# Third layer of a four-layer graph network: row factors spread by DMA instead of by TensorE transposes

## The chip, the cores and the metric

The kernel runs on 1 core of one Trainium2 chip. The metric is the device time in microseconds (us). Five engines work side by side, each with its own instruction stream: TensorE (PE in the profile, with PEld for its weight loads), VectorE (DVE), ScalarE (ACT), GpSimd (POOL) and SyncE (SP), which here only starts DMAs.

## The reference, cut to what matters

Sixteen graphs of 512 nodes with 128 features go through four attention layers, each followed by a residual sum and a layer norm. The third layer ("layer 2" in the names, L2 in the reference) has 8 heads of width 16:

```
e = leaky_relu(e_src[..., :, None] + e_dst[..., None, :], 0.2)
e = e + (beta * jnp.log(prior + EPS))[:, None, :, :]      # prior is the adjacency
e = jnp.where(adj > 0, e, neg_inf)
attn = softmax(e, axis=-1)
h = einsum('bhij,bhjf->bhif', attn, x_proj)               # 8 heads
return h.transpose(0, 2, 1, 3).reshape(B, N, D) @ W_out.T
```

The kernel never forms e. exp(leaky_relu(s_i + d_j)) is the larger of exp(s_i + d_j) and exp(0.2 (s_i + d_j)). After division by a factor that belongs to row i (it cancels in the softmax), a weight is max(R_i, T_j) times the mask, with R_i = exp(-0.8 (s_i + m)) and T_j = exp(0.8 (d_j - m)). A remaining factor of j is multiplied into the values. For each head one needs R as a row of 512 numbers that stands in all 128 partitions, since the nodes j lie along the partitions and the nodes i along the free dimension.

## The kernel before

Nodes lie as node = 4 p + c: 128 partitions, C = 4 columns of blocks. Everything is float32, but for the masks (bf16). Each stage is a small function of a graph `g` and a part; for each engine the string `ORDER[engine]` lists the stages as pairs of a letter and a graph number, and `turns` walks through it. So the order of work on every engine is written out as data, and an engine waits for its next stage even if a later one is ready. Four or five graphs are under way at once: while layer 0 of graph 9 runs, the same engines work on layer 1 of graph 8, layer 2 of graphs 7 and 6, and layer 3 of graphs 5 and 4. PSUM has 8 banks of 128 x 512; `BANK_OF_USE` gives the bank for each use, `wrote` and `took` are the waits for its being filled and emptied.

Layer 2 of one graph goes as follows:

- `l2_h` (TensorE, ScalarE) projects to 128 values and two scores for each of 8 heads. `l2_c4`, `l2_dm`, `l2_diag`, `l2_db` find the largest score m of each head, `l2_small` and `l2_cap` (VectorE) make the sums.
- `l2_e` (ScalarE, L758 to L760) makes R2 (the row factors, 128 x 32), t2e (the column factors T) and a factor for the values; `l2_scale` (GpSimd, L1292) multiplies the values by the latter.
- `l2_s` (TensorE, L561), once for each of 8 heads: four 128 x 128 transposes of a broadcast column of R2 spread the row factors of the head over all partitions of one PSUM bank.
- `l2_p` (VectorE, L1119), once for each head: four SCALAR_TENSOR_TENSOR of 128 x 512 make the weights P2 = max(row, T) x mask. P2 holds four heads, so head 4 waits for the product of the first four.
- `l2_v` (TensorE, L571), once for four heads: 16 matmuls of 128 x 512 with P2 as the moving operand. Then `l2_n`, `l2_rcp`, `l2_o`, `l2_oT`, `l2_y` normalise, project, and add the residual.

GpSimd does the elementwise work that needs no PSUM: `l0_bias` (L1229), `l1_y` (L1261), `scale` of the layers 1 and 3b (L1267), `l2_scale` (L1292), `below_zero` (L1274, `l3_min` on 128 x 1024 and `l3b_min` on 128 x 512), and after each layer norm's statistics four small instructions (`variance` L1237 and L1238, `power` L1245, `shifts` L1252) before ScalarE can normalise (L748). SyncE's queue starts one load of x (L398) and one store (L402) for each graph, in order, each after its wait.

## Time and profile before

| | |
|---|---|
| Device time, median of 3 runs | 1141.66 us (1140.52 to 1142.09) |
| The profiled execution: its own time, its span | 1140.98 us, 1139.2 us |
| Busy: PE, PEld, DVE, ACT, POOL | 1045.3, 782.5, 917.0, 736.3, 271.4 us |
| Mean TensorE clock granted | 0.977 of full |

The span runs from the first to the last instruction. Busy times are the union of an engine's instructions. A weight load overlaps the matmuls before it, so PE's busy time is what counts for the engine, with the idle time ahead of a group telling what it lacked. The profile names buffers without their numbers: `l_P` can be the weight matrix of layer 1 or of layer 3, and `bank` any PSUM bank.

### The profile page before, as it was taken

The numbers are of one execution on the slowest core, as the hardware profiler recorded it, in microseconds if no ns is written. First come the engines' busy times: TensorE is split into PE (matmuls) and PEld (weight loads), VectorE is DVE, ScalarE is ACT, GpSimd is POOL, SyncE is SP. The second block draws the span as 40 slices with busy tenths as digits, with TensorE's granted clock in tenths as the row PEclk, the third lists the DMA queues.
The fourth block names the chain that finished last, engine by engine and source line by source line (L and its number), as shares of the span: only waits on it lengthen the run. The fifth ranks groups of instructions, "written<-read, shape, count | busy, mean of one in ns | idle before, by whom it ended". The sixth has DMA issues, their size and how long they took to land. (4 is left out here: it accounts for less than half of the span.)

```text
span 1139.2 us, 26405 instructions
## 1 busy us (share of the span) xinstructions
PE 1045.3 (92%) x9333; PEld 782.5 (69%) x9333; DVE 917.0 (80%) x2514; ACT 736.3 (65%) x1901; POOL 271.4 (24%) x381
## 2 busy tenths in 40 slices
PE   2899999999999999999999999999999999879763
PEld 1567676877677767777787867777787768555552
DVE  4467999989897988979797997989797997977342
ACT  1699577757677684867678584867678584533522
POOL 0012212213131231413132141313132131421212
PEclk9999999999999999999999999999999999999877
DMA  4000000000000000000000000000000000000000
GB/s 120 1 11 12 11 2 11 1 11 11 10 2 12 10 11 11 11 11 11 11 2 11 10 11 11 11 11 11 11 1 11 2 11 2 10 1 10 10 0 19
DMA packets 9489, 12.97 MB, mean 11 GB/s; under 512 B 2704, under 2 KB 5008, under 8 KB 9232
## 3 DMA queue, kind: packets, MB, share of 16 engines
q1 hardware_dynamic: 9360, 11.28, 3.3%
q8 instruction: 77, 1.26, 0.5%
q14 instruction: 52, 0.43, 0.1%
HBM read 7.08 MB, written 4.19 MB: 10 GB/s over the span
## 5 line engine op out<-in xcount | busy, mean ns | idle before, releaser
L1119 DVE SCALAR_TENSOR_TENSOR P<-bank,t2e,mask_t 128x512 f32<-128x512 f32 x512 | 344.8, 739 | 19.1 <-PE bank L561 19.0
L703 ACT ACTIVATE probs<-probs,neg_max 128x512 f32<-128x512 f32 x256 | 184.8, 724 | 9.5 <-DVE neg_max L949 8.0
L748 ACT ACTIVATE x<-x,shift_l,rstd_l 128x128 f32<-128x128 f32 x256 | 105.6, 490 | 116.6 <-POOL shift_l L1252 116.4
L941 DVE CUSTOM_DVE_ANT_0 probs<-bank,mask_add 128x512 f32<-128x512 f32 x256 | 168.6, 677 | 15.3 <-PE bank L462 14.9
L713 ACT ACTIVATE probs_t<-bank 128x512 f32<-128x512 f32 x256 | 145.6, 614 | 10.4 <-PE bank L470 9.8
L470 PE MATMUL bank<-ident,probs 128*128 128x128 f32 x1024 | 139.6, 276 | 8.3 <-ACT probs_t L713 3.8
L470 PEld LDWEIGHTS bank<-ident,probs 128*128 128x128 f32 x1024 | 115.0, 141 | 28.9 <-ACT probs L703 15.2
L571 PE MATMUL bank<-P,GH 128*32 128x512 f32 x1024 | 119.7, 609 | 9.1 <-issue 8.2
L612 PE MATMUL bank<-t,l_P 128*128 128x257 f32 x512 | 121.2, 386 | 1.7 <-DVE l_P L1051 1.7
L612 PEld LDWEIGHTS bank<-t,l_P 128*128 128x128 f32 x512 | 94.6, 192 | 14.2 <-DVE l_P L1051 2.2
L571 PEld LDWEIGHTS bank<-P,GH 128*32 128x32 f32 x1024 | 32.2, 112 | 80.3 <-issue 78.9
L1274 POOL TENSOR_SCALAR e<-v 128x1024 f32<-128x1024 f32 x16 | 44.6, 2790 | 167.1 <-ACT v L795 155.7
L1237 POOL TENSOR_TENSOR rstd_l<-mv_l,ln_eps 128x4 f32<-128x4 f32 x64 | 12.8, 200 | 274.3 <-DVE mv_l L995 274.3
L539 PEld LDWEIGHTS bank<-t,l3b_P 128*128 128x128 f32 x512 | 63.5, 202 | 16.6 <-issue 10.1
L462 PE MATMUL bank<-head_k,head_q 32*128 32x512 f32 x512 | 73.7, 646 | 1.0 <-DVE row_max L941 0.5
L539 PE MATMUL bank<-t,l3b_P 128*128 128x129 f32 x512 | 67.6, 288 | 5.9 <-DVE l3b_P L1037 5.9
L1267 POOL TENSOR_TENSOR t<-t 128x512 f32<-128x512 f32 x32 | 33.4, 1045 | 150.0 <-ACT t L740 150.0
L539 PEld LDWEIGHTS bank<-t,l_P 128*128 128x128 f32 x512 | 59.6, 192 | 12.5 <-issue 10.9
L481 PEld LDWEIGHTS bank<-probs_t,v 128*32 128x32 f32 x2048 | 52.8, 110 | 21.9 <-issue 15.7
L1245 POOL TENSOR_TENSOR rstd_l<-rstd_l,neg_half 128x4 f32<-128x4 f32 x64 | 66.5, 1039 | 4.1
L481 PE MATMUL bank<-probs_t,v 128*32 128x128 f32 x2048 | 67.0, 275 | 0.5 <-issue 0.4
L561 PE MATMUL bank<-ident,R 128*128 128x128 f32 x512 | 66.0, 273 | 0.2
(161 smaller groups left out, 1944.2 us busy)
## 6 DMA issues: line engine op xcount, KB each, us to landing
x_in<-in_x SPq DMA_DIRECT2D x16, 256.0 KB, 3.0
out<-x SPq DMA_DIRECT2D x16, 256.0 KB, 2.0
l_P<-in_adj SPq DMA_DIRECT2D x1, 1024.0 KB, 5.1
w_fc<-in_L_gnn_W_fc SPq DMA_DIRECT2D x1, 256.0 KB, 3.5
probs_t<-in_L_gnn_a_fc SPq DMA_DIRECT2D x1, 256.0 KB, 5.6
w_cat<-in_L_gnn_W SPq DMA_DIRECT2D x2, 64.0 KB, 3.6
w3a<-in_L_gnn_mlp_w SPq DMA_DIRECT2D x1, 128.0 KB, 3.8
w3b<-in_L_gnn_mlp_w SPq DMA_DIRECT2D x1, 128.0 KB, 3.3
```

What stands on the lines that cost most here:

```text
L462: pe.matmul(ps("l0_s", g, HEADS0 * c + h)[:, :], g.of(head_q)[rows, c * P:(c + 1) * P], g.of(head_k)[rows, :], start=True, stop=True)\
L470: last = pe.transpose(ps[:, j * P:(j + 1) * P], probs[m // HEADS0 % 2][:, m % HEADS0, j * P:(j + 1) * P], ident[:, :])
L481: last = pe.matmul(ps[DH0 * h:DH0 * (h + 1), 0:P], g.of(v0)[:, j, DH0 * h:DH0 * (h + 1)], probs_t[c % 2][:, h, j, :], start=(j == 0), stop ...
L539: last = pe.matmul(ps[:, c * (D + 1):(c + 1) * (D + 1)], gat[n]["P"][:, j, (2 * k + c) * P:(2 * k + c + 1) * P], g.of(t)[:, j, 2:3 + D], s ...
L571: last = pe.matmul(ps[DH0 * h:DH0 * (h + 1), :], g.of(GH)[:, j, (GROUP2 * q + h) * W2:(GROUP2 * q + h) * W2 + DH0], P2[:, h, j, :], start= ...
L612: last = pe.matmul(ps[:, 0:HID + 1], gat["l3"]["P"][:, j, c * P:(c + 1) * P], g.of(t3)[:, j, 2:3 + HID], start=(j == 0), stop=(j == C - 1))
L703: act.activation(e, e, ACT.Exp, bias=neg_max[:, m:m + 1], scale=SCALE0, accum_out=g.of(den0)[:, m:m + 1])\
L713: act.activation(probs_t[c % 2][:, h, :, :].rearrange("p j n -> p (j n)"), ps("l0_t", g, m)[:, :], ACT.Copy)\
L748: last = act.activation(y[:, c, :], y[:, c, :], ACT.Identity, bias=shift[n][:, c:c + 1], scale=rstd[n][:, c:c + 1])
L941: dve.tensor_tensor_reduce(probs[c % 2][:, h, :], ps("l0_s", g, m)[:, :], mask_add[:, c, :], 1.0, -3.0e38, ALU.add, ALU.max, row_max[:, m: ...
L1119: last = dve.scalar_tensor_tensor(P2[:, h % GROUP2, j, :], ps("l2_s", g, h)[:, :], g.of(t2e)[:, j, h:h + 1], mask_t[:, j, :], ALU.max, ALU ...
L1245: pool.tensor_tensor(rstd[n][:, :], rstd[n][:, :], neg_half[:, :], ALU.pow)\
```

## The change

1. The stage `l2_s` is gone, with its 512 transposes and its 128 uses of a PSUM bank. In its place VectorE turns R2 in blocks of 32 x 32 (`l2_turn`, one instruction for each graph). SyncE's queue then writes the four blocks as 32 lines of 128 numbers to DRAM (`l2_rows`, four DMAs of 16 KB) and reads for each head 512 numbers back, once for every partition (`l2_spread`, eight DMAs of 256 KB into one of five buffers in SBUF, `row0` to `row4`). A head's spread waits for `l2_p` of five heads earlier.
2. `l2_p` reads the row factors from such a buffer in SBUF instead of from PSUM.
3. x3 has three buffers instead of two.
4. GpSimd's elementwise stages go in pieces of 128 columns: one instruction becomes four (eight for `l3_min`). The four small instructions of a layer norm stay as they are.
5. The order is new on all engines, and so are the banks.

```diff
+ROWS = 5
+BLOCK = 32
...
-        x1, x2, x3 = (pair(n, [P, C, D]) for n in ("x1", "x2", "x3"))
+        x1, x2, x3 = (pair(n, [P, C, D], n=k) for n, k in (("x1", 2), ("x2", 2), ("x3", 3)))
...
-        R2 = pair("R2", [P, HEADS2, C])
+        R2 = pair("R2", [P, HEADS2 * C])
+        turned2 = sb("turned2", [P, BLOCK])
...
+        rows = [sb(f"row{r}", [P, N_NODES]) for r in range(ROWS)]
...
+        line2 = [nc.dram_tensor(f"line2_{q}", [HEADS2 * C, P], F32, kind="Internal").ap() for q in range(2)]
...
+            def l2_rows(g, k):
+                sp.wait_ge(*sig("l2_turned", g, 1))
+                for q in range(0, P, BLOCK):
+                    sp.dma_start(g.of(line2)[:, q:q + BLOCK], turned2[q:q + BLOCK, :]).then_inc(signal["l2_rows"], 16)
+
+            def l2_spread(g, h):
+                if h == 0:
+                    sp.wait_ge(*sig("l2_rows", g, 64))
+                if HEADS2 * g.i + h >= ROWS:
+                    sp.wait_ge(signal["p2_made"], HEADS2 * g.i + h - ROWS + 1)
+                sp.dma_start(row(g, h)[:, :], g.of(line2)[h * C:(h + 1) * C, :].rearrange("c p -> (c p)")
+                             .rearrange("(o n) -> o n", o=1).broadcast_to([P, N_NODES])).then_inc(row_done(g, h)[0], 16)
...
-            def l2_s(g, h):
-                if h == 0:
-                    pe.wait_ge(*sig("exp2", g, 3))
-                ps = empty("l2_s", g, h)
-                for c in range(C):
-                    last = pe.transpose(ps[:, c * P:(c + 1) * P], g.of(R2)[:, h, c:c + 1].broadcast_to([P, P]), ident[:, :])
-                last.then_inc(filled("l2_s", g, h), 1)
...
-                pe.wait_ge(*took("l2_s", g, GROUP2 * q + GROUP2 - 1))
+                pe.wait_ge(*sig("p2_made", g, GROUP2 * (q + 1)))
...
+            def l2_turn(g, k):
+
+                dve.wait_ge(*sig("exp2", g, 1))
+                if g.has(1):
+                    dve.wait_ge(*sig("l2_rows", g, 64, back=1))
+                dve.transpose(turned2[:, :], g.of(R2)[:, :]).then_inc(signal["l2_turned"], 1)
+
             def l2_p(g, h):
-                dve.wait_ge(*wrote("l2_s", g, h))
+                dve.wait_ge(*row_done(g, h))
...
-                    last = dve.scalar_tensor_tensor(P2[:, h % GROUP2, j, :], ps("l2_s", g, h)[:, :], g.of(t2e)[:, j, h:h + 1],
+                    last = dve.scalar_tensor_tensor(P2[:, h % GROUP2, j, :], row(g, h)[:, :], g.of(t2e)[:, j, h:h + 1],
                                                     mask_t[:, j, :], ALU.max, ALU.mult)
-                last.then_inc(emptied("l2_s", g, h), 1)
+                last.then_inc(signal["p2_made"], 1)
...
-                    pool.tensor_scalar(e[:, :, :], v(g)[:, :, :], 0.0, None, ALU.min).then_inc(signal[n + "_min"], 1)
+                    for c in range(C):
+                        for q in range(0, e.shape[2], P):
+                            last = pool.tensor_scalar(e[:, c, q:q + P], v(g)[:, c, q:q + P], 0.0, None, ALU.min)
+                    last.then_inc(signal[n + "_min"], 1)
```

In the steady part of the program TensorE's rows change as follows. Before, the spreads of the row factors (L561, here of graph 7) stand between attention products of layer 3 (L612), of layer 3b (`l3b_P`) and the products of layer 2 (L571).

```order
495 L571 MATMUL bank<-P,GH 32x512 x16
496 L539 MATMUL bank<-t_0,l3b_P 128x129 x8
497 L553 MATMUL bank<-dmax_diag,ones 128x8
498 L612 MATMUL bank<-t_0,l_P 128x257 x4
499 L433 MATMUL bank<-ident,x_1 128x128 x4
500 L561 MATMUL bank<-ident,R_0 128x128 x4
501 L539 MATMUL bank<-t_0,l3b_P 128x129 x8
502 L462 MATMUL bank<-head_k,head_q 128x512 x4
503 L579 MATMUL bank<-ident,o_raw 128x128 x4
504 L561 MATMUL bank<-ident,R_0 128x128 x4
505 L612 MATMUL bank<-t_0,l_P 128x257 x8
506 L561 MATMUL bank<-ident,R_0 128x128 x8
```

Now, in the period of the same graphs (L592 is the product of layer 2, L633 the attention product of layer 3, L491 the scores of layer 0):

```order
450 L582 MATMUL bank<-dmax_diag,ones 128x8
451 L491 MATMUL bank<-head_k,head_q 128x512 x4
452 L556 MATMUL bank<-ident,l3b_R 128x128 x4
453 L592 MATMUL bank<-P,GH 32x512 x16
454 L462 MATMUL bank<-ident,x_1 128x128 x4
455 L633 MATMUL bank<-t_0,l_P 128x257 x4
456 L538 MATMUL bank<-w_cat,xTl 128x130 x2
457 L633 MATMUL bank<-t_0,l_P 128x257 x8
458 L491 MATMUL bank<-head_k,head_q 128x512 x4
```

The rows of L561 have no successor; the other stages are the same ones in another order.

On VectorE, before, the small sums of graph 7 (L1102 to L1107) are followed almost at once by the first weights P:

```order
805 L1102 TENSOR_TENSOR small<-t_0,dmax_all 128x32
806 L1103 TENSOR_TENSOR small<-t_0,dmax_all 128x32
807 L1107 TENSOR_SCALAR small<-small 128x32
808 L1145 RECIPROCAL l_rden<-bank 128x1
809 L1119 SCALAR_TENSOR_TENSOR P<-bank,t2e,mask_t 128x512 x4
```

Now the turn of the row factors (STREAM_TRANSPOSE) and other work stand between them:

```order
823 L1128 TENSOR_SCALAR small<-small 128x32
824 L1072 TENSOR_SCALAR l_P<-bank,l_g,l_b 128x512
825 L1136 STREAM_TRANSPOSE turned<-R_1 128x32
826 L1072 TENSOR_SCALAR l_P<-bank,l_g,l_b 128x512
827 L962 ISA probs,row_max<-bank,mask_add 128x512
828 L962 ISA row_max 128x1
829 L1058 SCALAR_TENSOR_TENSOR l3b_P<-bank,l3b_b,mask_t 128x512
830 L970 TENSOR_SCALAR neg_max<-row_max 128x4
831 L1058 SCALAR_TENSOR_TENSOR l3b_P<-bank,l3b_b,mask_t 128x512 x2
832 L1173 RECIPROCAL l_rden<-bank 128x1
833 L1058 SCALAR_TENSOR_TENSOR l3b_P<-bank,l3b_b,mask_t 128x512
834 L1173 RECIPROCAL l_rden<-bank 128x1
```

The next row is the first P of graph 7, from `row`. The last four heads of the graph stand later in the period, close together, with a layer norm of layer 1 started just ahead of them (BN_AGGR):

```order
888 L1016 BN_AGGR mv_l<-stats_l 128x2 x4
889 L962 ISA probs,row_max<-bank,mask_add 128x512
890 L962 ISA row_max 128x1
891 L1147 SCALAR_TENSOR_TENSOR P<-row,t2e,mask_t 128x512 x4
892 L1196 TENSOR_TENSOR x_0<-x_0,bank 128x512
893 L970 TENSOR_SCALAR neg_max<-row_max 128x4
894 L1147 SCALAR_TENSOR_TENSOR P<-row,t2e,mask_t 128x512 x4
895 L1202 SCALAR_TENSOR_TENSOR x_0<-x_0,x_1 128x512
896 L1147 SCALAR_TENSOR_TENSOR P<-row,t2e,mask_t 128x512 x4
```

SyncE's queue, which held one load and one store for each graph, now holds twelve DMAs more for each, in one line with them:

```order
66 L423 DMA line_0<-turned 32x32 x4
67 L430 DMA row<-line_0 128x512 x8
68 L418 DMA out<-x_1 128x512
69 L414 DMA x_in<-in_x 128x512
70 L423 DMA line_1<-turned 32x32 x4
71 L430 DMA row<-line_1 128x512 x8
```

## Rows read from the trace of the kernel before

**Rows 1.** Windows: each engine's busy time (its instructions), PEclk, DMA share, GB/s

```profile
0.00:200.00 200.00, 167.82 (x1708) 117.38 (x1709) 144.63 (x427) 136.64 (x363) 31.74 (x61) 0.99 0.09 24
200.00:960.00 760.00, 747.07 (x6875) 568.84 (x6874) 664.13 (x1819) 531.25 (x1376) 197.59 (x269) 1.00 0.03 9
960.00:1139.20 179.20, 130.37 (x755) 96.33 (x753) 108.23 (x270) 68.40 (x163) 42.03 (x52) 0.86 0.02 8
```

**Rows 2.** Windows: one period of the steady part, and another, later

```profile
398.00:462.70 64.70, 63.42 (x584) 48.29 (x583) 56.47 (x156) 45.69 (x119) 17.10 (x24) 1.00 0.03 10
...
656.80:721.50 64.70, 63.42 (x585) 48.25 (x583) 56.46 (x158) 45.69 (x120) 17.09 (x24) 1.00 0.03 10
```

**Rows 3.** Groups by line and form: busy us, mean ns | idle before, releaser

```profile
L1119 DVE SCALAR_TENSOR_TENSOR P<-bank,t2e,mask_t 128x512 f32<-128x512 f32 x512 | 344.8, 739 | 19.1 <-PE bank L561 19.0
...
L941 DVE CUSTOM_DVE_ANT_0 probs<-bank,mask_add 128x512 f32<-128x512 f32 x256 | 168.6, 677 | 15.3 <-PE bank L462 14.9
...
L561 PE MATMUL bank<-ident,R 128*128 128x128 f32 x512 | 66.0, 273 | 0.2
...
L1051 DVE TENSOR_SCALAR l_P<-bank,l_g,l_b 128x512 f32<-128x512 f32 x64 | 50.5, 795 | 1.5 <-PE bank L527 1.1 <-issue 0.4
L1037 DVE SCALAR_TENSOR_TENSOR l3b_P<-bank,l3b_b,mask_t 128x512 f32<-128x512 f32 x64 | 46.7, 743 | 2.8 <-ACT t L740 1.5 <-PE bank L527 1.3
...
L1145 DVE RECIPROCAL l_rden<-bank 128x1 f32<-128x1 f32 x64 | 10.4, 162 | 26.8 <-PE bank L612 26.7
```

**Rows 4.** Timeline (start us, us), VectorE and TensorE, two stretches

```profile
642.18 1.47 PE L561 MATMUL bank<-ident,R 128*128 128x128 f32 x12
...
647.30 2.72 DVE L1119 SCALAR_TENSOR_TENSOR P<-bank,t2e,mask_t 128x512 f32<-128x512 f32 x4
...
654.30 0.69 DVE L1174 SCALAR_TENSOR_TENSOR x<-x 128x512 f32<-128x512 f32 x1
654.90 0.23 DVE L1023 TENSOR_SCALAR l_dd<-t,l_ndmax 128x4 f32<-128x4 f32 x1
```

**Rows 5.** Timeline, VectorE and GpSimd, 660 to 663 us

```profile
660.50 1.28 POOL L1229 TENSOR_TENSOR x_in<-x_in,bias_o 128x512 f32<-128x512 f32 x1
...
660.65 2.20 DVE L1150 SCALAR_TENSOR_TENSOR v<-e,v 128x1024 f32<-128x1024 f32 x1
...
661.73 1.18 POOL L1252 TENSOR_TENSOR shift_l<-shift_l,rstd_l 128x4 f32<-128x4 f32 x1
...
662.78 0.68 DVE L941 CUSTOM_DVE_ANT_0 probs<-bank,mask_add 128x512 f32<-128x512 f32 x1
```

**Rows 6.** Single lines: durations in ns, min/median/max, first and last start

```profile
L1150 DVE SCALAR_TENSOR_TENSOR v<-e,v x16: 1205/2046/2209, 216.6 to 1104.7; 128x1024 f32<-128x1024 f32 x16
...
L1252 POOL TENSOR_TENSOR shift_l<-shift_l,rstd_l x64: 198/200/1198, 69.9 to 1134.8; 128x4 f32<-128x4 f32 x64
...
L1245 POOL TENSOR_TENSOR rstd_l<-rstd_l,neg_half x64: 1006/1018/2159, 68.8 to 1133.7; 128x4 f32<-128x4 f32 x64
...
L1119 DVE SCALAR_TENSOR_TENSOR P<-bank,t2e,mask_t x512: 648/741/753, 107.0 to 1042.1; 128x512 f32<-128x512 f32 x171
```

**Rows 7.** Groups by line and form, GpSimd's two sizes of one operation

```profile
L1274 POOL TENSOR_SCALAR e<-v 128x1024 f32<-128x1024 f32 x16 | 44.6, 2790 | 167.1 <-ACT v L795 155.7 <-DVE v L928 11.4
...
L1274 POOL TENSOR_SCALAR e<-x 128x512 f32<-128x512 f32 x16 | 23.9, 1492 | 74.5 <-issue 71.1 <-ACT x L804 3.4
```

**Rows 8.** Timeline of SyncE's queue at the start: DMAs issued one behind another

```profile
10.59 0.43 SPq L367 DMA_DIRECT2D probs_t<-in_L_gnn_a_src  x1
11.07 0.43 SPq L367 DMA_DIRECT2D probs_t<-in_L_gnn_a_dst  x1
11.54 0.44 SPq L367 DMA_DIRECT2D probs_t<-in_L_gnn_a_fc  x1
```

**Rows 9.** DMA issues: KB each, median us from issue to landing

```profile
x_in<-in_x SPq DMA_DIRECT2D x16, 256.0 KB, 3.0
out<-x SPq DMA_DIRECT2D x16, 256.0 KB, 2.0
...
probs_t<-in_L_gnn_a_fc SPq DMA_DIRECT2D x1, 256.0 KB, 5.6
...
probs_t<-in_L_gnn_a_dst SPq DMA_DIRECT2D x1, 64.0 KB, 5.2
```

**Rows 10.** Timeline near the end: TensorE waits for the weights P

```profile
1023.87 5.63 PE L571 MATMUL bank<-P,GH 128*32 128x512 f32 x32 [5.70 <-issue]
```

## What the change will do to the time

> **What bounds the kernel now.** I read the busy times by stage first. In the long middle TensorE works 747.1 of 760 us, in the first 200 us 167.8, in the last 179.2 us 130.4 [rows 1]. So it idles 32.2 us at the start, 12.9 in the middle and 48.8 at the end, 93.9 in all. Then one period: graphs follow each other every 64.7 us, TensorE is busy 63.4 of them, VectorE 56.5, ScalarE 45.7, GpSimd 17.1 [rows 2]. The reader is to see that TensorE sets the period, with 1.3 us of idle time, and that VectorE comes 7 us behind it. The middle holds 760 / 64.7 = 11.75 periods. The groups by line say what TensorE's time is made of: the spreads of the row factors (L561) take 66.0 us, with hardly any idle time ahead, so they are work and not waits [rows 3]; the timeline has 12 of them in 1.47 us, 0.12 each [rows 4]. By graph that is 66.0 / 16 = 4.1 us.
>
> **What goes from TensorE.** All 512 transposes of L561, 66.0 us; nothing is added. TensorE then has 1045.3 - 66.0 = 979.3 us of work, and 63.4 - 4.1 = 59.3 in a period. In the middle, where TensorE sets the pace, this is a gain until something else is slower than 59.3.
>
> **What VectorE gets.** Its 32 instructions of `l2_p` for each graph now read two tensors from SBUF. Before, four of them last 2.72 us, and a single one 0.74, so one follows another at (2.72 - 0.74) / 3 = 0.66 us. The nearest row with both tensors in SBUF, of the same operation and size (L1174), starts at 654.30 and the next instruction at 654.90: 0.60 us [rows 4]. I take 0.60, and 32 x 0.06 = 1.9 us less in a graph; the bound on the other side is no saving. The turn of 128 x 32 has no row; small instructions of VectorE such as L1145 take 0.16 us, 0.80 is the price of 512 columns (L1051) [rows 3], and I take 0.3. The sum of layer 3 (L1150) took 2.05 us at the median and 1.2 at best [rows 6], because of GpSimd (below); with short pieces it should lose 0.3 instead of 0.8, so 0.5 less. VectorE alone: 56.5 - 1.9 + 0.3 - 0.5 = 54.4 us.
>
> **The port.** This is what can eat the gain. At 660.50 GpSimd starts a sum of 1.28 us (L1229) that ends at 661.78. VectorE starts L1150, with two inputs in SBUF, at 660.65. It ends at 662.85, 1.07 us after GpSimd's end, hardly less than its whole 1.2: it stood still meanwhile. And GpSimd's next, a sum of 128 x 4 that takes 0.20 elsewhere, starts at 661.73 and ends at 662.91, with L1150 [rows 5, 6]. So an instruction of VectorE with two SBUF inputs and one of GpSimd go one after the other. Before, `l2_p` has one input in SBUF, and its 512 instructions never took over 0.753 us [rows 6]. Now they get into this. The Trainium skill, page "SBUF — State Buffer", section "Who interferes with whom", says the same as a rule: a VectorE instruction with two SBUF inputs contends with a GpSimd instruction that reads SBUF, and the second to start is blocked for the whole of the first. The rows agree for L1150; for `l2_p` no row can. By the skill's rule alone the change is a loss of time on VectorE wherever the two meet.
>
> How much? GpSimd's 17.1 us grow by the pieces. 1024 columns take 2.79 us and 512 take 1.49 [rows 7], so 2.5 ns a column and 0.19 us for each instruction. There are 7 + 3 + 5 x 3 = 25 instructions more in a graph, 0.15 to 0.19 each: about 4.3 us, and GpSimd comes to some 21.4 us. VectorE's instructions with two SBUF inputs fill 32 x 0.60 + 1.2 + 2 x 0.6 = 21.6 us, 36% of a period of 60. Laid evenly, 0.36 x 21.4 = 7.7 us of GpSimd meet them. If VectorE pays for all of it: 7.7 us. If GpSimd always waits: 0. The order shows both kinds of places: from the small sums to the first P the rows hold none of `l2_p`, while the last four heads stand tight behind a layer norm, whose GpSimd steps then come among them. I take 3.5 us, just under half, since a piece that waits for the end of a P costs only GpSimd, which has time.
>
> **The DMAs.** Between the turn and the first P of the same graph VectorE has, from the order, one L1051 (0.8), one L941 (0.7), four L1037 (4 x 0.73) and three small ones (0.5) [rows 3]: 4.9 us. In this time the queue must issue four DMAs, 0.48 us apart (1.4 to the start of the last) [rows 8], wait for its landing (2.0, as the store), issue the spread and wait for that (3.0, as the load of the same 256 KB) [rows 9]: 6.4 us. The first head is late by 1.5 us. The nearest spread rows, loads of one line to all partitions, took up to 5.6 us [rows 9], but with others ahead of them in the queue; with 5.6 the lateness is 4.1, and with 2.0 for both landings 0.5. The later heads are not late: the buffers hold five, and spreads can follow at 0.48 us while a head takes 2.4. Behind the waiting P stand, on VectorE, the scores of layer 0 and all else in its order, for which ScalarE waits, so I count 1.5 us on VectorE in full. The queue itself has 12 DMAs more, 12 x 0.48 = 5.8 us of 60. A load or store behind them waits for some us more; in the order x of a graph is loaded two graphs ahead, so this costs nothing. The bytes, 8 x 256 KB a graph, are 34 GB/s on top of the 9 there now [rows 1]; one load of 256 KB in 3.0 us is already 87 GB/s, so I cost them at nothing too.
>
> **The rest.** The third x3 buffer removes a wait that no row shows; nothing. The pieces lengthen GpSimd's own stages (`l3_min` by 1.1 us) on chains that have slack in the middle. At the end they have not.
>
> **The sum.** TensorE 59.3 us; VectorE 54.4 + 1.5 + 3.5 = 59.4. The two are level. With orders written out, a wait of either one is not made up for by the other, and a period is longer than both: before, with 7 us between them, TensorE idled 1.3. I take 2.2: a period of 61.5. Middle: 11.75 x 2.2 = 26 us of idle TensorE. Start: 33 (32.2 before). End: 48.8 now; there TensorE waits 5.7 us for P at 1023.87 [rows 10], so the transposes that go leave idle time in part, and two late first heads and longer GpSimd stages come on top; I take 54. Span: 979.3 + 33 + 26 + 54 = 1092.3, and 1.8 us lie around it (1140.98 - 1139.2): 1094. Against the profiled execution's 1141.0 that is 47 us less (4.1%); this execution lies within 0.1% of the median of 1141.66.
>
> **The rivals.**
> - The full gain: the port costs VectorE little, and idle times stay as they are. 979.3 + 93.9 + 1.8 = 1075 us. For it: VectorE keeps 5 us of room even before the port. Against: L1150 pays on each meeting. Chance 0.18.
> - VectorE becomes the bound: the port costs it 6 us. 54.4 + 1.5 + 6 = 61.9, with 1.3 on top 63.2, so TensorE idles 3.9 x 11.75 = 46: 979.3 + 33 + 46 + 54 + 1.8 = 1114. For it: the 7.7 us of an even spread. Chance 0.15.
> - No change: the two meet so often that the period stays at 64.7, 1141. Chance 0.03.
> - Slower, through the port alone: before each P a GpSimd piece gets in. It decides from 64.7 - 1.3 - 55.9 = 7.5 us a graph on VectorE, about 16 pieces of 0.46 (0.19 + 128 x 2.5 ns) with 32 P to stand before. All 21.4 us of GpSimd can't meet P, but 11 could: 66.9 + 1.3 = 68.2 a period, 3.5 x 11.75 = 41 us more than now, 1182. Against: in long stretches of the new order no P stands. This is what the skill's rule (same page and section) would give if GpSimd were always the first to start. Chance 0.07.
> - My forecast, with a port price of 2 to 5 us: chance 0.57, from 1082 to 1106.
>
> **Numbers.** 1094 us. The range leaves out the slower cases and the end of the full gain: 1073 to 1122. Less than 0.2% can't be told here, as the three runs lie 0.14% apart. Faster 0.90, same 0.03, slower 0.07.
>
> **What would show it.** TensorE's busy time at 979 (more, if the clock falls in the gaps). A period of 61.5. `l2_p` with a minimum near 0.68 us as a single one and a tail above 1 us, where the blocked ones are; their number times the excess over 0.6 is the port's price, 3.5 us a graph. Waits of VectorE on the spread DMA, at the first head alone, 1.5 us each. L1150 near 1.5. GpSimd's busy time near 340 us or above, as its waits count as busy. The prediction is wrong if rows of `l2_p` are blocked in most cases, if the spreads take 5 us each, or if an order that no longer fits makes TensorE wait on ScalarE, which has 14 us of room.

## The result and the profile after

The changed kernel takes 1126.77 us (1126.14 to 1128.36, 4 runs) where the kernel before took 1141.22 (4 runs on the same chip): a ratio of 0.9875, 95% interval 0.9858 to 0.9892. It is 14.4 us faster; 47 us were forecast, and 1127 lies above the range. The profiled execution of after has a span of 1125.1 us.

Windows of after, the same stages as [rows 1], then two steady periods as [rows 2] (busy time of PE, PEld, DVE, ACT, POOL with their instructions, granted clock, DMA share, GB/s):

```profile
0.00:200.00 200.00, 160.16 (x1593) 108.80 (x1594) 142.23 (x421) 134.83 (x355) 48.10 (x102) 0.98 0.15 45
200.00:960.00 760.00, 728.13 (x6645) 539.52 (x6647) 684.28 (x1880) 540.79 (x1408) 298.75 (x585) 1.00 0.14 45
960.00:1125.10 165.10, 109.41 (x590) 79.23 (x582) 90.94 (x230) 58.72 (x141) 50.28 (x96) 0.83 0.06 22
...
487.50:549.00 61.50, 59.85 (x554) 44.17 (x555) 56.45 (x156) 45.56 (x119) 24.50 (x49) 1.00 0.14 45
673.90:736.80 62.90, 60.27 (x554) 44.19 (x555) 56.09 (x156) 45.20 (x119) 24.45 (x49) 1.00 0.14 44
```

TensorE is busy 997.7 us instead of 1045.3, not 979.3 as forecast, and idle 39.8 + 31.9 + 55.7 = 127.4 us instead of 93.9. A period is 61.5 to 62.9 us; seven of them, from 425.8 to 860.0 by the reciprocal spreads of layer 0 (`l0_rd`), average 62.0. TensorE's share of one fell by 3.4 us (63.4 to 60.0), VectorE's stayed at 56.

Single lines of after, as [rows 6]: P (L1147) with VectorE's waits ahead of it (us, times), and layer 3's sum (L1178, L1150 before):

```profile
L1147 DVE SCALAR_TENSOR_TENSOR P<-row,t2e,mask_t x512: 652/743/950, 109.7 to 1028.3; 128x512 f32<-128x512 f32 x171
...
  DMA row<-line: 15.3, 10
...
L1178 DVE SCALAR_TENSOR_TENSOR v<-e,v x16: 1204/1210/1226, 223.4 to 1088.3; 128x1024 f32<-128x1024 f32 x16
```

A group of after, GpSimd's `l3_min` as the first of [rows 7], and from its DMA issues the spread rows (KB each, median us to landing), as [rows 9]:

```profile
L1308 POOL TENSOR_SCALAR e<-v 128x128 f32<-128x128 f32 x128 | 77.4, 632 | 171.2 <-ACT v L816 171.2
```

```profile
row<-line SPq DMA_DIRECT2D x128, 256.0 KB, 3.7
```

P from SBUF takes what it took from PSUM, 743 ns at the median against 741. Its tail reaches 950 instead of 753. Where it meets GpSimd's pieces both stretch. Here is a costly meeting of a period, as start and duration in us (four P without a GpSimd piece beside them take 2.73 us here, 2.72 in [rows 4]):

```profile
522.42 3.33 DVE L1147 SCALAR_TENSOR_TENSOR P<-row,t2e,mask_t 128x512 f32<-128x512 f32 x4
...
522.56 3.50 POOL L1258 TENSOR_TENSOR x_in<-x_in,bias_o 128x128 f32<-128x128 f32 x4 [1.26 <-PE bank L462]
```

VectorE lost 0.6 us there and GpSimd 1.8 (four pieces without P take 1.69, as a row of an experiment below shows). P's busy time is 358.6 us against 344.8: the port costs VectorE at most 13.8 us in all, 0.9 a graph, and 3.5 were forecast. L1178, which took 2.05 us because of GpSimd, is back at 1.21. VectorE waits for rows ten times, 15.3 us in all.

By `l0_rd` of graph 6 (367.1 before, 364.3 after) the start has gained 2.7 us; the next nine periods gain 19.2 (579.1 to 559.9, or 64.3 to 62.2 each); from `l0_rd` of graph 15 to the end 7.9 are lost again (193.0 to 200.8). The mark stands at another place among the stages in the new order, so the parts are less certain than their sum.

### The profile page after: what moved, and what is told of

It reads as the page before. It is cut to its first block, busy times and chain, and to the rows that moved or that the text cites. A ratio compares the mean times of both kernels' runs of the same rounds, so it can differ in the third digit from the quotient of the medians.

```text
span 1125.1 us, 26002 instructions
## 1 busy us (share of the span) xinstructions
PE 997.7 (89%) x8821; PEld 727.6 (65%) x8821; DVE 917.5 (82%) x2530; ACT 734.3 (65%) x1901; POOL 397.1 (35%) x781
## 4 chain that ended last, share of the span: by engine, by line
PE 34%; DVE 25%; issue 8%; POOL 4%; ACT 3%; DVEq 0%; ACTq 0%; POOLq 0%
DVE P L1147 15%; PE bank L633 8%; PE bank L592 7%; PE bank L491 4%; PE bank L538 2%; POOL e L1308 2%; DVE stats_l L1006 2%; PE bank L470 2%; PE bank L499 2%; DVE l_P L1058 1%; ACT x L769 1%; PE bank L462 1%; DVE v L1178 1%; POOL rstd_l L1274 1%; DVE h_t L1183 1%
## 5 line engine op out<-in xcount | busy, mean ns | idle before, releaser
L1147 DVE SCALAR_TENSOR_TENSOR P<-row,t2e,mask_t 128x512 f32<-128x512 f32 x512 | 358.6, 760 | 18.3 <-DMA row<-line 15.3
L734 ACT ACTIVATE probs_t<-bank 128x512 f32<-128x512 f32 x256 | 149.2, 601 | 10.8 <-PE bank L499 10.8
L499 PE MATMUL bank<-ident,probs 128*128 128x128 f32 x1024 | 137.4, 275 | 13.9 <-ACT probs L724 12.6
L769 ACT ACTIVATE x<-x,shift_l,rstd_l 128x128 f32<-128x128 f32 x256 | 105.3, 483 | 62.9 <-POOL shift_l L1281 62.8
L1308 POOL TENSOR_SCALAR e<-v 128x128 f32<-128x128 f32 x128 | 77.4, 632 | 171.2 <-ACT v L816 171.2
L1266 POOL TENSOR_TENSOR rstd_l<-mv_l,ln_eps 128x4 f32<-128x4 f32 x64 | 19.3, 302 | 298.2 <-DVE mv_l L1016 298.1
L592 PE MATMUL bank<-P,GH 128*32 128x512 f32 x1024 | 117.4, 599 | 5.5 <-DVE P L1147 2.8
L633 PE MATMUL bank<-t,l_P 128*128 128x257 f32 x512 | 119.1, 383 | 1.1 <-DVE l_P L1072 1.1
L633 PEld LDWEIGHTS bank<-t,l_P 128*128 128x128 f32 x512 | 94.7, 191 | 16.2 <-issue 2.4
L491 PE MATMUL bank<-head_k,head_q 32*128 32x512 f32 x512 | 74.5, 645 | 5.6 <-DVE h_t L1183 2.6
L592 PEld LDWEIGHTS bank<-P,GH 128*32 128x32 f32 x1024 | 30.9, 110 | 74.6 <-issue 70.9
L1299 POOL TENSOR_TENSOR t<-t 128x128 f32<-128x128 f32 x128 | 50.3, 423 | 69.1 <-ACT t L761 69.1
L1274 POOL TENSOR_TENSOR rstd_l<-rstd_l,neg_half 128x4 f32<-128x4 f32 x64 | 69.2, 1082 | 5.0
L1258 POOL TENSOR_TENSOR x_in<-x_in,bias_o 128x128 f32<-128x128 f32 x64 | 45.2, 736 | 67.8 <-PE bank L462 67.8
L568 PE MATMUL bank<-t,l_P 128*128 128x129 f32 x512 | 64.2, 281 | 3.4 <-DVE l_P L1058 3.3
```

The lines of the kernel that those rows point to most:

```text
L491: pe.matmul(ps("l0_s", g, HEADS0 * c + h)[:, :], g.of(head_q)[rows, c * P:(c + 1) * P], g.of(head_k)[rows, :], start=True, stop=True)\
L499: last = pe.transpose(ps[:, j * P:(j + 1) * P], probs[m // HEADS0 % 2][:, m % HEADS0, j * P:(j + 1) * P], ident[:, :])
L568: last = pe.matmul(ps[:, c * (D + 1):(c + 1) * (D + 1)], gat[n]["P"][:, j, (2 * k + c) * P:(2 * k + c + 1) * P], g.of(t)[:, j, 2:3 + D], s ...
L592: last = pe.matmul(ps[DH0 * h:DH0 * (h + 1), :], g.of(GH)[:, j, (GROUP2 * q + h) * W2:(GROUP2 * q + h) * W2 + DH0], P2[:, h, j, :], start= ...
L633: last = pe.matmul(ps[:, 0:HID + 1], gat["l3"]["P"][:, j, c * P:(c + 1) * P], g.of(t3)[:, j, 2:3 + HID], start=(j == 0), stop=(j == C - 1))
L734: act.activation(probs_t[c % 2][:, h, :, :].rearrange("p j n -> p (j n)"), ps("l0_t", g, m)[:, :], ACT.Copy)\
```

## The experiments

Two theories. By the prediction, TensorE's work sets the pace until VectorE does. The other says that some ring of waits through several engines' queues is as long as a period or longer, so that work pays where the ring runs through it. Each kernel was compared with the kernel before on its chip, which took 1138.5 to 1140.3 us in those sets; a difference to the changed kernel or between sets is one of medians, and uncertain by up to 3 us. No run has the new order with the transposes kept, or with two x3 buffers, so the share of the order and that of the rows by DMA are not separated.

### Parts of the change taken out

**GpSimd whole again** in the changed kernel:

```diff
-                    for c in range(C):
-                        for q in range(0, e.shape[2], P):
-                            last = pool.tensor_scalar(e[:, c, q:q + P], v(g)[:, c, q:q + P], 0.0, None, ALU.min)
-                    last.then_inc(signal[n + "_min"], 1)
+                    pool.tensor_scalar(e[:, :, :], v(g)[:, :, :], 0.0, None, ALU.min).then_inc(signal[n + "_min"], 1)
```

and so for the four other stages.

> The changed kernel (1126.8 us) with GpSimd's elementwise stages in one instruction each, as before. Theory: GpSimd's pieces and its meetings with the weights P are a small part of what was lost; VectorE's P instructions run 14 us longer in all than before, and the first and last stretches lose time through the order. Then 1120 to 1132: the chains through GpSimd get 1.1 us shorter per stage, P is blocked longer where it meets a whole stage (up to 2.8 us). Rival, the pieces are what costs (GpSimd 397 us busy against 271): 1112 or less. Rival, the pieces save the port from worse: 1140 or more, with P instructions of up to 3 us.

Measured: 1137.97 us, ratio 0.9987 (0.9970 to 1.0005). The pieces are worth 11 us in the new order. P took 367.0 us (358.6 in pieces), the longest one 1.77 us (0.95), and the seven periods average 63.2 us instead of 62.0. Other parts are worth as much when they are taken out (below), so these prices do not add up to the 14.4 us and are no shares of it.

**P reads one fixed tile**, no rows by DMA (it leaves out the row factors): `row(g, h)` becomes `fixed_row`, without `l2_turn`'s wait, `l2_rows` and `l2_spread`.

> The changed kernel without the DMAs of the row factors: P reads one fixed tile in SBUF, so its values are not the reference's, and SyncE's queue has only loads and stores. Everything else, the order too, stays. Rival theory, late rows are what was lost: the 15.3 us that VectorE waited for them come back in full, 1111 or less. Theory (the order and its ends): the waits move to the next thing in line, and 1118 to 1126 remain.

Measured: 1119.79 us, ratio 0.9824 (0.9806 to 0.9842), 7.0 us under the changed kernel. Of the 15.3 us of waits for rows about half were on the path. P kept its 0.66 us from one to the next (358.8 us busy), so it is not the transfers that hold it there.

**The kernel before with one transpose of four** (it leaves out three quarters of the row factors): `for c in range(C)` in `l2_s` becomes `range(1)`.

> The kernel before, in its old order, with one of the four transposes for each head left out three times: 384 transposes less, so three quarters of the row factors stay what the bank held. It shows what TensorE's time alone is worth in the old order. 384 x 0.11 us = 42 us: theory, 1141 - 42 = 1099, perhaps 1102 with the last stretch bound by others. If another engine becomes the bound at once, 1115 or more. Either way the period says how much of the 2.6 us of now was to be had.

Measured: 1136.51 us, ratio 0.997 (0.996 to 0.998). 384 transposes went, 42 us at 0.11 each; TensorE's busy time fell by 26, since a transpose by itself costs more than one of four, and the time by 2.7. Windows of two periods:

```profile
428.60:492.71 64.11, 62.00 (x567) 45.69 (x563) 56.35 (x156) 45.53 (x118) 17.06 (x23) 1.00 0.03 9
492.71:557.29 64.58, 61.12 (x566) 45.25 (x561) 56.50 (x156) 45.57 (x118) 17.33 (x23) 1.00 0.03 10
```

Seven periods (those of the same graphs as above) average 64.3 us instead of 64.5, while TensorE's busy time in one fell from 63.4 to 61.9. So in the old order TensorE's work did not set the period.

**Old order, heads 0 and 1 by transposes, heads 2 to 7 by DMA** with six buffers, GpSimd whole, two x3 buffers.

> The old order, with heads 0 and 1 still spread by transposes and heads 2 to 7 by DMA from the turned factors (six buffers), GpSimd whole, x3 with two buffers. 384 transposes are gone as in the quarter kernel, but with the DMAs and with P reading SBUF for six heads. Theory (the new order is what lost the time at both ends): near the quarter kernel, 1100 to 1110. Rival (DMA or port): 1120 or more, with waits on the row DMA or P instructions far above 0.74 us.

Measured: 1169.16 us, ratio 1.0264 (1.0249 to 1.0280). VectorE waited only 0.6 us for rows. Two other things show in the trace. VectorE is busy 933.4 us instead of 917.0, since GpSimd's whole stages hold P up (773 ns on average from SBUF, 743 from PSUM, and 1.77 us at the longest). And P holds up the layer norm's small steps on GpSimd (four P at 562.92 take 2.71 us); undisturbed these are 0.20, 0.20 and 1.02. No run separates the two. Rows of the second:

```profile
563.08 0.62 POOL L1363 TENSOR_TENSOR rstd_l<-mv_l,ln_eps 128x4 f32<-128x4 f32 x1 [2.48 <-DVE mv_l L1114]
563.65 0.71 POOL L1364 TENSOR_TENSOR shift_l<-mv_l,neg_one 128x4 f32<-128x4 f32 x1
564.44 1.40 POOL L1371 TENSOR_TENSOR rstd_l<-rstd_l,neg_half 128x4 f32<-128x4 f32 x1
565.91 0.20 POOL L1378 TENSOR_TENSOR shift_l<-shift_l,rstd_l 128x4 f32<-128x4 f32 x1
566.15 1.65 ACT L867 ACTIVATE x<-x,shift_l,rstd_l 128x128 f32<-128x128 f32 x4 [2.39 <-POOL shift_l L1378]
```

ScalarE stands still for 2.39 us behind them.

### What a microsecond of each engine is worth

**A constant as P's scalar** instead of `g.of(t2e)[:, j, h:h + 1]`, first in the changed kernel, then in the kernel before (it leaves out the column factors in the maximum).

> The changed kernel with a constant 0.75 as the scalar of the third layer's maximum instead of the column of target factors (the values of that layer are wrong; every instruction and transfer is still there). Two questions. First the cadence: if the scalar read through a pointer is what keeps four of these operations at 2.73 us from SBUF, they fall to about 2.5 (cadence 0.60); if the masks or the output set it, they stay at 2.73. Second, if they do fall, 384 x 0.06 = 31 us leave VectorE. Theory that VectorE and TensorE alternate on one chain (513.6 to 529.9 VectorE, 529.9 to 534.7 TensorE in the trace of after): about half comes back, 1108 to 1117. Rival that TensorE alone now sets the period: 1124 to 1128. Rival that VectorE is the bound: 1096 to 1102.

> The same constant in the kernel before, whose maximum reads its rows from PSUM. If the pointer sets the cadence, four take about 2.5 us here too; if PSUM sets it, they stay at 2.73, and then the same edit must fall short only here. In time: if the old order's periods wait on a chain through VectorE, as the removal of three quarters of the transposes suggested (2.7 us for 42 us of TensorE work), 31 us less VectorE is worth 10 to 25 us, 1115 to 1130. Rival that a period of the old order is set by its own order of waits whatever one engine saves: 1136 to 1140.

Measured: 1116.20 us, ratio 0.9798 (0.9783 to 0.9813), and 1135.36, ratio 0.9958 (0.9942 to 0.9973). The medians of P, from SBUF and then from PSUM:

```profile
L1147 DVE SCALAR_TENSOR_TENSOR P<-row,mask_t x512: 628/683/954, 109.5 to 1016.8; 128x512 f32<-128x512 f32 x171
```

```profile
L1119 DVE SCALAR_TENSOR_TENSOR P<-bank,mask_t x512: 626/681/692, 106.3 to 1034.0; 128x512 f32<-128x512 f32 x171
```

The scalar read from SBUF costs 0.06 us an instruction, the PSUM source nothing: the step from 0.60 to 0.66 was the scalar's. VectorE lost 25 to 27 us of work; the time fell by 10.6 in the new order, as the theory of an alternating chain would have it, and by 4.9 in the old, just below its rival's range.

**8 of 16 groups of layer 0's transposes done twice** in the changed kernel:

```diff
-                for j in range(C):
+                for j in range(C) if m % 2 else [0, 1, 2, 3, 0, 1, 2, 3]:
```

> The changed kernel with 8 of each graph's 16 groups of first-layer transposes done twice into the same bank (same output): 8 x 0.44 = 3.5 us more TensorE work a graph, 56 us in all, about what the change took away. Theory that TensorE, busy 60.0 of 62.0 us of a period, is close behind the chain in the new order: the 2.0 us of idle time take up part and the rest is paid, 1150 to 1170. Rival that TensorE is the bound at once: 1175 to 1185. Rival that it isn't near the bound, as in the old order, where 2.6 us a graph less was worth 0.2: 1128 to 1140.

Measured: 1142.02 us, ratio 1.0025 (1.0013 to 1.0038). TensorE's busy time rose by 44.9 us, the run's by 15.3. In a period it is now busy without a gap, and seven periods (434.8 to 873.7) average 62.7 us, 0.7 more:

```profile
434.77:497.24 62.47, 62.44 (x591) 47.76 (x587) 56.34 (x156) 45.86 (x118) 23.96 (x49) 1.00 0.15 44
497.24:559.67 62.43, 62.39 (x590) 47.76 (x585) 56.41 (x156) 46.06 (x118) 23.99 (x49) 1.00 0.14 44
```

That is just above the rival's range and under the theory's. Read backwards, and as far as work at this place stands for work at another, it prices the change's own saving: of the 3.4 us a period that TensorE gave back, the last 2.4 bought 0.7.

**Pieces in the kernel before**, nothing else.

> The kernel before with GpSimd's five elementwise stages in pieces of 128 columns, and nothing else of the change. In the new order the pieces were worth 11 us (1138 whole, 1127 in pieces). Theory that whole stages hold the maximum up wherever both meet: here too some us, 1128 to 1136. Rival that the pieces matter only where the maximum reads and writes SBUF alone and meets the stages by the new order: 1139 to 1145, since each GpSimd stage becomes longer by the starts of its pieces.

Measured: 1164.75 us, ratio 1.0219 (1.0202 to 1.0236). Both expectations missed: 24 us slower, 1.5 a graph. From `l3_min`'s start to the norm's shift GpSimd's run of stages grew from 7.5 to 9.2 us (461.67 to 469.13 before, 467.56 to 476.78 here). This pointed at the ring.

### The ring of the old order

Timeline of the kernel before, GpSimd, ScalarE, VectorE and TensorE in turn (start and duration in us; in brackets the idle time before and what ended it):

```profile
526.11 3.03 POOL L1274 TENSOR_SCALAR e<-v 128x1024 f32<-128x1024 f32 x1 [11.40 <-DVE v L928]
...
529.41 1.04 POOL L1267 TENSOR_TENSOR t<-t 128x512 f32<-128x512 f32 x1
530.41 1.03 POOL L1245 TENSOR_TENSOR rstd_l<-rstd_l,neg_half 128x4 f32<-128x4 f32 x1
531.42 1.27 POOL L1229 TENSOR_TENSOR x_in<-x_in,bias_o 128x512 f32<-128x512 f32 x1
532.65 1.18 POOL L1252 TENSOR_TENSOR shift_l<-shift_l,rstd_l 128x4 f32<-128x4 f32 x1
...
533.87 1.65 ACT L748 ACTIVATE x<-x,shift_l,rstd_l 128x128 f32<-128x128 f32 x4 [2.13 <-POOL shift_l L1252]
...
535.62 0.69 DVE L975 TENSOR_TENSOR x<-bank,x 128x512 f32<-128x512 f32 x1 [0.62 <-ACT x L748]
...
539.93 1.65 ACT L748 ACTIVATE x<-x,shift_l,rstd_l 128x128 f32<-128x128 f32 x4 [0.58 <-POOL shift_l L1252]
...
541.63 0.66 PE L433 MATMUL bank<-ident,x 128*128 128x128 f32 x4 [1.42 <-ACT x L748]
```

`l3_min` of one graph stands in GpSimd's queue ahead of the last norm of the graph before it, with `l1_scale` (L1267) and `l0_bias` (L1229) between. ScalarE waits for that norm's shift. VectorE's sum of layer 2 (L975) waits for the norm, since it writes the x3 buffer of two graphs earlier. Its own norm then lets TensorE start layer 3 of the next graph (L433), which ends in the next `l3_min`. [rows 5] are the middle of it, read there as a meeting on a port only. The order of the stages is read from the queues; that this ring sets the period is for the following runs to show.

**A third x3 buffer** in the kernel before: `pair("x3", [P, C, D], n=3)`, and `x3_free` looks back three graphs.

> The kernel before with a third x3 buffer and nothing else. The trace of before shows one ring that goes round once a period: l3_min on GpSimd (526.11 to 529.1), behind it in GpSimd's queue l3_var, l1_scale, l3_pow, l0_bias and l3_shift of the graph before (to 533.8), ScalarE's norm (533.87 to 535.5), VectorE's sum l2_y at 535.62, which waited 0.62 us because two x3 buffers make it wait for that norm, its statistics, GpSimd, ScalarE at 539.93, TensorE at 541.63 after 1.42 us idle, and on to the next l3_min. Theory of the ring: with a third buffer l2_y waits no more and TensorE's work (63.4 of 64.7 us) becomes the bound: about 1 us a period, 1122 to 1132. Rival that the ring isn't what holds the period: 1138 to 1142.

Measured: 1132.70 us, ratio 0.9948 (0.9933 to 0.9963), just outside what the ring was to give: 5.8 us from a part that the prediction cost at nothing. VectorE's wait is gone; ScalarE's for the shift stays.

**The third buffer and one transpose of four** (it leaves out three quarters of the row factors).

> The same with one of the four transposes of each third-layer row block (it leaves out three quarters of the row factors, as the run with one transpose of four in the kernel before did, where 42 us less of TensorE's work was worth 2.7 us). Theory of the ring: with the ring open the same work is worth 20 to 35 us more, 1090 to 1112. Rival that another chain through VectorE holds the old order: no more than 5 us below the third buffer alone.

Measured: 1127.25 us, ratio 0.9900 (0.9885 to 0.9915), 5.4 us below the buffer alone, not 20 to 35. The reading is that cutting one of the two waits does not open the ring, since ScalarE's, through its in-order queue, holds all behind it; the runs with both cuts, below, bear on it.

**`l0_bias` behind `l3_shift`** in the kernel before, ten periods:

```diff
-    l3_min, l3_var, l1_scale, l3_pow, l0_bias, l3_shift
+    l3_min, l3_var, l1_scale, l3_pow, l3_shift, l0_bias
```

> The kernel before with GpSimd's l0_bias put behind l3_shift instead of between l3_pow and l3_shift, in the ten periods where it stood there. Theory of the ring: it takes 1.2 to 1.3 us out of it in ten periods of 16, about 8 to 12 us, until TensorE's work stops it at about 1 us a period: 1127 to 1133. Rival: 1140.

Measured: 1125.92 us, ratio 0.9886 (0.9870 to 0.9903). One instruction of GpSimd, moved by one place, in each of ten periods, gives 12.6 us, a little more than expected and nearly as much as the whole change. GpSimd and ScalarE at the same place, then a period of it:

```profile
518.99 3.02 POOL L1286 TENSOR_SCALAR e<-v 128x1024 f32<-128x1024 f32 x1 [11.40 <-DVE v L940]
...
524.40 0.20 POOL L1264 TENSOR_TENSOR shift_l<-shift_l,rstd_l 128x4 f32<-128x4 f32 x1
524.55 2.27 POOL L1241 TENSOR_TENSOR x_in<-x_in,bias_o 128x512 f32<-128x512 f32 x1
...
524.63 1.65 ACT L760 ACTIVATE x<-x,shift_l,rstd_l 128x128 f32<-128x128 f32 x4
```

```profile
489.05:552.25 63.20, 63.17 (x590) 47.88 (x586) 55.41 (x156) 45.57 (x118) 17.35 (x23) 1.00 0.03 10
```

The shift ends 5.6 us after the start of `l3_min` (7.7 before; 1.3 were `l0_bias`, 1.0 the shift itself, which layer 3's sum no longer holds up), ScalarE does not wait, and TensorE is busy 63.17 of 63.20 us. Only now is its work the bound. (VectorE's sum of layer 3, L1150 before, also takes 1.22 instead of 2.20 us at this place, since it now goes first and holds up `l0_bias` instead. That is 8 us less of VectorE's work in the run, and 27 us less were worth 4.9 in this order, so it is a small part of the 12.6.)

**Both cuts, with and without the transposes** (the first leaves out three quarters of the row factors).

> The kernel before with both cuts of the ring, the third x3 buffer and l0_bias behind l3_shift, and one of the four transposes of each third-layer row block (it leaves out three quarters of the row factors). Moving l0_bias alone left TensorE busy 63.2 of 63.2 us of a period; TensorE's work alone cut to 61.0 left the period at 63.9 with the third buffer. Theory that the old order's period is the longer of the ring through GpSimd's queue and TensorE's work: with both cut the period falls to 61 to 62, which is worth 11 to 20 us against the two cuts alone, 1100 to 1112. Rival that some other ring stands at 63 us: 1117 to 1124.

> The two cuts of the ring with all transposes (full computation). By the theory TensorE's 63.2 us is then the bound: no more than 3 us below the move of l0_bias alone, 1122 to 1126. If the two cuts add up (5.8 and 12.6 us), 1119 to 1122.

Measured: 1119.15 us, ratio 0.9817 (0.9802 to 0.9831), and 1124.12, ratio 0.9864 (0.9848 to 0.9881). The two cuts do not add up, as the theory said. But the transposes brought 5.0 us where 11 to 20 were expected. TensorE's busy time fell by 1.7 us a period, to 61.3, and the period by 0.4:

```profile
423.70:486.10 62.40, 61.52 (x566) 45.52 (x562) 55.40 (x156) 45.57 (x118) 17.12 (x23) 1.00 0.03 10
486.10:549.00 62.90, 61.08 (x566) 45.26 (x562) 55.42 (x156) 45.62 (x118) 17.37 (x23) 1.00 0.03 10
```

A third limit stands at about 62.7 us, the mean of these two periods, and what it runs through was not found.

**The rows by DMA in the old order**, all heads, five buffers, both cuts, GpSimd whole.

> The kernel before with both cuts of the ring, and all eight row blocks of each graph by VectorE's turn and DMA into five row buffers instead of by transposes, in the old order of every engine, GpSimd's stages whole. The cuts alone gave 1124, with TensorE busy 62.9 to 63.2 of it a period; this takes 3.4 us of TensorE's work out of a period. Theory that the row blocks by DMA pay once the ring is cut: 1105 to 1118. Rival by the mixed run (two heads by transposes, six by DMA, 1169 without the cuts): maximum and GpSimd's stages hold each other up in the ring, and it ends above the cuts alone, 1126 to 1155.

Measured: 1255.76 us, ratio 1.1029 (1.1010 to 1.1047), far outside both. In the old order the first P follows the turn at once:

```profile
559.62 0.21 DVE L1245 STREAM_TRANSPOSE turned<-R 128x32 f32<-128x32 f32 x1
565.81 2.74 DVE L1257 SCALAR_TENSOR_TENSOR P<-row,t2e,mask_t 128x512 f32<-128x512 f32 x4 [5.99 <-DMA row<-line]
```

```profile
DVE P L1257 <- DMA row<-line: 98.7, 16, 7.5
```

The second fence is the row of its waits (us in all, times, longest): 16 waits of 6.2 us on average: the way through DRAM takes 6.2 us from the turn's start, and here nothing covers it. The waits are 99 of the 132 us that this kernel is slower than the two cuts alone; VectorE's busy time is up too (931.4 us instead of 907.8), and TensorE's clock falls behind the waits:

```profile
557.50 2.00 PE L743 MATMUL bank<-t,l_P 128*128 128x257 f32 x8
...
569.28 6.65 PE L743 MATMUL bank<-t,l_P 128*128 128x257 f32 x16 [5.90 <-DVE row_max L1072]
```

In the stretch from 568.4 to 575.2, after TensorE had been idle for 5.9 us, the granted clock is 0.50, the lower level of 1.2 GHz. Eight of these matmuls take 2.00 us at the full clock, and 16 take 6.65 here. In the old order the rows by DMA do not pay; the new order puts other work between the turn and the first P, and 15.3 us of waits are left.

### The new order

**`l0_bias` back between `l3_pow` and `l3_shift`** in the changed kernel.

> The changed kernel with l0_bias put back between l3_pow and l3_shift of the graph six before, everything else of the change kept. Theory of the ring: the third x3 buffer has opened it, so the place costs little, 1125 to 1131, and what GpSimd's order gains there isn't the cause of the result. Rival that GpSimd's new order is worth most of the 14 us: 1136 to 1145.

Measured: 1137.41 us, ratio 0.9993 (0.9973 to 1.0013), 10.6 us above the changed kernel; the rival was right. The shift of the norm comes 1.7 us later, behind `l0_bias`, and ScalarE waits twice as long for it as in the changed kernel (1.54 us at 489.14); TensorE waits 1.50 us soon after:

```profile
490.74 1.69 POOL L1270 TENSOR_TENSOR x_in<-x_in,bias_o 128x128 f32<-128x128 f32 x4
492.39 0.20 POOL L1293 TENSOR_TENSOR shift_l<-shift_l,rstd_l 128x4 f32<-128x4 f32 x1
...
492.62 1.65 ACT L781 ACTIVATE x<-x,shift_l,rstd_l 128x128 f32<-128x128 f32 x4 [3.09 <-POOL shift_l L1293]
...
494.98 0.32 PE L559 MATMUL bank<-ident,l_dmax 128*128 128x128 f32 x1 [1.50 <-DVE l_dmax L1038]
```

**Minima in pieces of a row block** (256 and 128 columns): `e[:, c, :]` in one instruction.

> The changed kernel with the minimum of the third layer's output and of the last layer's in pieces of one row block (256 and 128 columns) instead of 128 throughout: four pieces for the larger instead of eight. The eight take 5.00 us where they meet the maximum (510.92 in the trace of after) and 2.8 whole. If GpSimd's queue is part of the ring in the new order too, as the return of l0_bias to its old place there (+11 us) suggests, 1 us less of it a period is worth 3 to 10 us, 1117 to 1124. Rival that longer pieces hold the maximum up as long as they save: 1126 to 1131.

Measured: 1127.11 us (1123.98 to 1133.24), ratio 0.9894 (0.9860 to 0.9928): no difference that these runs tell.

**The reciprocals of layer 0 ahead of the last P** of a graph, nine periods:

```diff
-    l2_p, l0_den, l3_aggr, l0_rcp
+    l0_den, l3_aggr, l0_rcp, l2_p
```

> The changed kernel with l0_den, l3_aggr and l0_rcp ahead of a graph's last maximum instead of behind it, in nine periods. In the trace of after VectorE is busy without a gap from 505.7 to 548.9, and waits 1.2 us for l0_rd and 1.25 us for l0_y after it. If VectorE's stretch is what the period waits for there, one of the waits is filled, 1 us a period, 1115 to 1121. Rival that TensorE, which waits only 0.26 us for the reciprocals, reaches that point late by itself: 1124 to 1128.

Measured: 1119.43 us, ratio 0.9818 (0.9804 to 0.9833), 7.3 us below the changed kernel and the best kernel here that computes all. Two periods, and the place:

```profile
424.20:485.10 60.90, 59.50 (x558) 44.15 (x552) 56.28 (x157) 45.42 (x118) 25.82 (x49) 1.00 0.14 45
485.10:546.10 61.00, 59.61 (x565) 44.28 (x557) 56.35 (x157) 45.55 (x118) 25.95 (x49) 1.00 0.14 45
```

```profile
547.20 0.69 DVE L1024 TENSOR_TENSOR o_t<-bank,o_raw 128x512 f32<-128x512 f32 x1 [0.71 <-PE bank L554]
```

VectorE's wait for `l0_rd` fell from 1.19 to 0.71 us here; the one for `l0_y` behind it stayed at 1.25.

**The first P behind two maxima of layer 0** on top of that.

> The reordered kernel of the run before (l0_den, l3_aggr and l0_rcp ahead of the last maximum), and each graph's first maximum behind the next l3_rcp, l1_c4 and two l0_max in nine periods. There VectorE waits for the first row block's transfer: 0.8 to 2.6 us in six of nine periods, 1.4 on average. The two l0_max can't start before their scores are there (504.4 where the maximum stood at 503.4). Theory that the late transfer is on the chain of the new order: it gains where the wait is over 1 us, 1112 to 1118. Rival that l3_rcp and what ScalarE makes of it, and the first maximum itself, come later by as much: 1119 to 1124.

Measured: 1146.10 us, ratio 1.0070 (1.0049 to 1.0091), 27 us slower, beyond the rival too. VectorE in that place:

```profile
511.46 0.17 DVE L1241 RECIPROCAL l_rden<-bank 128x1 f32<-128x1 f32 x1 [1.56 <-PE bank L701]
513.65 0.16 DVE L1094 TENSOR_REDUCE l_dmax<-t 128x1 f32<-128x4 f32 x1 [2.02 <-ACT t L816]
...
515.05 2.74 DVE L1215 SCALAR_TENSOR_TENSOR P<-row,t2e,mask_t 128x512 f32<-128x512 f32 x4
```

The P had filled the time in which VectorE waits for these two; the waits are open now, 3.6 us, and P comes behind them. What the move was made for did come about: VectorE's waits for rows fell from 15.0 us in ten to 5.9 in three.

## Why the prediction was wrong

- **The step that failed: "In the middle, where TensorE sets the pace, this is a gain until something else is slower than 59.3."** Busy 63.4 of 64.7 was read as the bound. In the old order the ring through GpSimd's queue and ScalarE set the period: 26 us less of TensorE's busy time gave 3, one GpSimd instruction moved 12.6, and with that TensorE's work became the bound at 63.2. What the change took from TensorE is 3.4 us a period; in the new order the last 2.4 of these bought 0.7, by the run with more work.
- **Where the miss lies.** Nine steady periods were to gain 9 x 3.2 = 28.8 us and gained 19.2. The other 18.1 of the forecast's 46.9 us of span were to come from the start and the end, and these lost 5.2 together (2.7 gained, 7.9 lost). So 23.3 of the 32.8 us that are missing lie there. The sum took the transposes out of these stretches in full as well, though TensorE was busy only 130.4 of the last 179.2 us. From the same mark to the end it is 200.8 us in the changed kernel, 202.7 without the rows' DMAs and 198.2 with GpSimd whole: neither accounts for the 7.9 us, and what in the new order does stays open.
- **Levels.** The steady period itself was nearly right, 61.5 forecast and 62.0 measured, but that is luck: not for its reason, and from 64.7, which the nine periods did not hold (64.3). "The two are level" expected VectorE at 59.4, 1.5 of it waiting; it has 56.3 and 1.0 of waiting. The new order has a limit of its own. It answers to GpSimd's order (`l0_bias`, 10.6 us), VectorE's (7.3 by one move) and TensorE's work, and its path was not traced.
- **The sum.** 32.8 us of span are missing: 18.4 in the term for TensorE's work, 14.4 in the idle terms (6.8 at the start, 5.9 in the middle, 1.7 at the end). The work term took 66.0 us from the groups, whose overlap counts twice: a group of four shows 0.60 us, the next starts 0.44 after it (12 transposes in 1.47 us [rows 4]), and 128 x 0.44 = 56.3 is what goes. That is 9.7 of the 18.4. Of the other 8.7 about 4 are the clock, by an estimate: TensorE is busy 38.7 us at half the clock in the changed kernel and 30.6 in the kernel before (0.83 and 0.86 are the mean clocks from 960 us on), and half of the 8.1 us more is added length. The prediction named this ("more, if the clock falls in the gaps") and put no number to it. The rest was not traced.
- **"The third x3 buffer removes a wait that no row shows; nothing."** A row did: L975 waits 0.62 us a period, and the buffer alone gave 5.8 us in the old order; in the new one it was not tried. A small wait at the end of a ring shows what the ring is short by, not what it costs.
- **Pieces "on chains that have slack in the middle."** They had none in the old order, 24 us slower. In the new one, where P meets GpSimd's stages, the pieces are 11 us faster, which goes with P being held up less (busy 358.6 us against 367.0) and not with slack.
- **P's cadence of 0.60.** The row was read rightly and does not match: L1174 has a constant as its scalar, and P one read from SBUF. P stayed at 0.66, so the 1.9 us a graph were not there.
- **The port, 3.5 us a graph.** VectorE paid 0.9. "A piece that waits for the end of a P costs only GpSimd, which has time" is the wrong half: GpSimd pays more than VectorE, and ScalarE stands behind it. The Trainium skill, page "SBUF — State Buffer", section "Who interferes with whom", has the second of the two blocked for the whole of the first. The traces agree: with GpSimd whole the longest P takes 1.77 us. In pieces the two go by turns, instruction by instruction, and the longest P is 950 ns, 0.2 above the undisturbed. The forecast for L1150 erred the other way: 0.5 us less was expected, and it fell from 2.05 to 1.21.
- **The rows by DMA.** 1.5 us for each first head, 24 in all, were forecast as paid in full; 15.3 were waited and 7.0 paid. The latency of 6.2 us is near the 6.4 worked out, from landings of 1.5 and 3.7 us at the median where 2.0 and 3.0 were taken. (The four DMAs of `l2_rows` are 4 KB each, 16 KB together.)

## What to carry to other kernels

With the order written out for each queue, an engine busy 98% of a period need not be the bound: follow one wait of it back through the other queues for a whole period, and test it by moving the shortest instruction on that path before removing work from the busy engine. A step between two halves of a layer norm, on an engine busy a quarter of the time, was worth nearly as much here as the whole change with its 512 transposes. A DMA that replaces work of an engine brings its latency (6.2 us here), and is worth what other work the order can put over it.

## What the runs showed of the hardware

- The per-partition scalar of SCALAR_TENSOR_TENSOR read from SBUF costs 0.06 us in 0.74, and whether a 128 x 512 float32 source is in PSUM or SBUF makes no difference (681 and 683 ns with a constant, 741 and 743 without).
- Where VectorE (two SBUF inputs) and GpSimd meet, GpSimd's four pieces went from 1.69 to 3.50 us and VectorE's four from 2.73 to 3.33.
- In the kernel with 99 us of waits for rows, TensorE's granted clock was at its lower level (0.50, 1.2 GHz) for 6.8 us behind 5.9 us of idle time. Over the run the mean clock was 0.93, and the same 8821 matmuls took 1038.9 us instead of 997.7 at 0.97.
